# Attention scores of two heads in the two row halves of TensorE, the gate copied out of PSUM, and operand stacks written through DRAM

## What is computed

```python
q, k, v = proj(Wq, bq, layernorm(x)), proj(Wk, bk, ctx), proj(Wv, bv, ctx)
q, k = rope(q, d_rope), rope(k, d_rope)          # the first 8 of each head's 16 channels are rotated
scores = jnp.einsum('bhqd,bhkd->bhqk', q, k) / jnp.sqrt(jnp.float32(kc))
p_attn = jax.nn.softmax(scores, axis=-1)
out = jnp.einsum('bhqk,bhkd->bhqd', p_attn, v)
x = x + proj(Wo, bo, out)
# feed-forward on layernorm(x)
gate = bitlinear(x, w_gate)                      # 512 -> 2048, act_quant(x) @ ternary weights
up = bitlinear(x, w_up)
intermediate = jax.nn.silu(gate) * up
return h_bitlinear(intermediate, w_down)         # Walsh-Hadamard over 2048, act_quant, 2048 -> 512
```

## Time and profile before

| | |
|---|---|
| time, median of 3 runs | 1619.53 us (1617.6 to 1630.68) |
| profiled execution, its own time | 1624.36 us |
| its span, first to last instruction | 1622.6 us |
| busy over the span | TensorE 91%, VectorE 81%, ScalarE 69%, GpSimd 52% |
| mean granted TensorE clock | 0.971 of full speed; full from about 180 us on |
| share of the DMA engines | about 0.3 |

### The profile page before, as it was taken

The page is one execution under the profiler, slowest core; times in us unless marked ns, Lnnn a source line. Parts: engine busy times, 40 slices in busy tenths (PEclk is TensorE's granted clock), DMA queues, the critical chain, the costliest instruction groups (busy, mean ns, idle before and its releaser), DMA issues.

```text
span 1622.6 us, 26340 instructions
## 1 busy us (share of the span) xinstructions
PE 1481.5 (91%) x8579; PEld 666.8 (41%) x8674; DVE 1318.3 (81%) x2317; ACT 1125.9 (69%) x1841; POOL 848.4 (52%) x648
## 2 busy tenths in 40 slices
PE   1378999999999999999999999999999999999984
PEld 0112344444444444444444434444444444444433
DVE  4477988888888888888888888888888888888741
ACT  4436677777777777777777777777777777777662
POOL 0111665555556655555556655555566555555464
PEclk9568999999999999999999999999999999999997
DMA  5633312233333233223332322323332322333000
GB/s 195 167 111 59 56 44 56 54 57 57 66 66 64 42 59 59 55 56 62 66 66 46 60 56 55 58 56 66 66 64 42 63 53 56 57 50 53 14 7 14
DMA packets 79750, 99.50 MB, mean 61 GB/s; under 512 B 9472, under 2 KB 59904, under 8 KB 78592
## 3 DMA queue, kind: packets, MB, share of 16 engines
q1 hardware_dynamic: 79056, 93.62, 30.1%
q10 hardware_dynamic: 560, 4.19, 0.7%
HBM read 38.80 MB, written 8.39 MB: 29 GB/s over the span
## 4 chain that ended last, share of the span: by engine, by line
PE 75%; DVE 12%; issue 3%; POOL 3%; ACT 2%; DMA 2%; SPq 1%; POOLq 0%; DVEq 0%; ACTq 0%
PE pv L468 15%; PE s L453 14%; PE ring L498 13%; PE s L425 12%; PE ring L543 6%; PE ring L397 6%; PE ring L519 4%; DVE maxima L989 3%; PE ring L477 2%; PE ring L530 2%; DVE h_res L1020 1%; DVE st L1022 1%; DVE attn L1009 1%; DVE turned_pv L999 1%; POOL region L1222 1%
## 5 line engine op out<-in xcount | busy, mean ns | idle before, releaser
L989 DVE TENSOR_REDUCE maxima<-s 128x1 bf16<-128x512 f32 x1024 | 667.0, 683 | 119.9 <-PE s L425 117.8
L688 ACT ACTIVATE region<-s 128x512 f32<-128x512 f32 x1024 | 575.2, 597 | 208.1 <-PE s L453 167.4
L1221 POOL TENSOR_TENSOR region<-region 128x512 f32<-128x512 f32 x192 | 253.3, 1319 | 391.3 <-DVE region L1069 363.8
L425 PE MATMUL s<-region 96*128 96x512 bf16 x1024 | 374.0, 390 | 26.0 <-DMA region<-parts 15.8
L453 PE MATMUL s<-region 97*128 97x512 bf16 x1024 | 352.8, 384 | 5.5 <-ACT region L688 3.0
L468 PE MATMUL pv<-region,v_ext 128*32 128x512 f32 x2048 | 267.2, 605 | 0.5 <-DVE turned_pv L999 0.4
L1222 POOL TENSOR_TENSOR region<-region 128x512 f32<-128x512 f32 x192 | 245.4, 1278 | 0.0
L453 PEld LDWEIGHTS s<-region 97*128 97x128 bf16 x1024 | 95.9, 98 | 240.0 <-ACT region L688 121.2
L425 PEld LDWEIGHTS s<-region 96*128 96x128 bf16 x1024 | 97.6, 97 | 205.8 <-DVE maxima L989 74.7
L1256 POOL TENSOR_TENSOR region<-region,parts 128x1024 f32<-128x1024 f32 x32 | 68.1, 2129 | 175.1 <-ACT parts L755 175.1
L704 ACT ACTIVATE region<-ring 128x512 f32<-128x512 f32 x128 | 76.2, 596 | 116.1 <-PE ring L509 116.1
(11 more groups left out here) (113 smaller groups left out, 1858.1 us busy)
## 6 DMA issues: line engine op xcount, KB each, us to landing
region<-parts SPq DMA_DIRECT2D x768, 64.0 KB
x_in<-in_x SPq DMA_DIRECT2D x32, 256.0 KB, 2.6
c_in<-in_ctx SPq DMA_DIRECT2D x32, 256.0 KB, 2.9
x_res<-in_x SPq DMA_DIRECT2D x32, 256.0 KB, 4.0
out<-o_sb SPq DMA_DIRECT2D x32, 256.0 KB, 4.1
region<-in_wg_t ACTq DMA_DIRECT2D x1, 2048.0 KB, 10.6
region<-in_wu_t SPq DMA_DIRECT2D x1, 2048.0 KB, 7.4
region<-in_wd_t SPq DMA_DIRECT2D x1, 2048.0 KB, 14.8
```

Of the source, the lines that this page charges most:

```text
L425: pe.matmul(s1[p][:, :], q_stack[k][0:STACK, h, 128 * c:128 * (c + 1)], k_stack[k][0:STACK, h, :], start=True, stop=True).then_inc(s1_full ...
L688: act.activation(probs[:, n % 8, :], s2[n % 2][:, :], ACT.Exp, scale=SCALE).then_inc(exp_done, 1)
L989: dve.reduce_max(maxima[:, c, h:h + 1], s1[p][:, :], AXX).then_inc(s1_max[p], 1)
L1221: pool.tensor_tensor(o[:, :, 0, :], a[:, :, 0, :], a[:, :, 1, :], ALU.add)
```

## The change

**Row halves.** The heads are paired, an even one (p = 0) and an odd one (p = 1). Its operands lie in rows 0 to 63 for the even and in rows 64 to 127 for the odd head. 64 rows hold four of the six terms (main); the other two terms and the maximum lie in 33 rows of a second column block (rest). `score_max(b, i)` is now a pair of matmuls with 64 rows each, one for each head, into both banks `s1`; it uses the four main terms. `scores(b, m)` is a pair over the main rows and a pair over the rest rows that accumulates onto it, into both banks `s2`. A pair waits until both banks have been read. There are 16 of each a unit.

**Gate.** ScalarE copies a quarter of the gate out of PSUM (`gate_out`), VectorE's `glu` multiplies only up with 1 + tanh, and GpSimd multiplies the two (`gate_product`).

**Stacks.** SP writes each part to a DRAM tensor `scratch` (6 DMAs a unit) and reads from there (12 DMAs a unit, 6 main and 6 rest) into the stacks.

**Weights and order.** up is loaded beside gate, into other buffers. Rounding is on VectorE (one instruction a piece) and the ternary step is ScalarE's Sign; the two steps of clipping are gone. All lists `step(t)` are new, and so is the ring's order.

```diff
-            def score_max(b, n):
-                if not live(b):
-                    return
-                k, p, i = slot(b), n % 2, n // 2
-                h, c = 2 * (i // KC) + p, i % KC
-                if n == 0:
-                    pe.wait_ge(stacked, 16 * STACK_DMAS * (b + 1))
-                wait(pe, s1_max[p], 16 * b + i)
-                pe.matmul(s1[p][:, :], q_stack[k][0:STACK, h, 128 * c:128 * (c + 1)],
-                          k_stack[k][0:STACK, h, :], start=True, stop=True).then_inc(s1_full[p], 1)
+            def score_max(b, i):
+
+                if not live(b):
+                    return
+                k, c = slot(b), i % KC
+                if i == 0:
+                    pe.wait_ge(main_stacked, 16 * READS_MAIN * (b + 1))
+                for p in range(2):
+                    wait(pe, s1_max[p], 16 * b + i)
+                j = i // KC
+                for p in range(2):
+                    pe.matmul(s1[p][:, :], q_stack[k][main_rows(p), j, 128 * c:128 * (c + 1)],
+                              k_stack[k][main_rows(p), j, :], start=True, stop=True).then_inc(s1_full[p], 1)
...
-            def scores(b, n):
+            def scores(b, m):
...
+                k, u = slot(b), m // 2
+                j, c = 2 * (u // KC) + m % 2, u % KC
...
-                wait(pe, exp_done, 32 * b + n - 1)
-                pe.matmul(s2[n % 2][:, :], k_stack[k][0:STACK + 1, h, 128 * c:128 * (c + 1)],
-                          q_stack[k][0:STACK + 1, h, :], start=True, stop=True).then_inc(s2_full, 1)
+                wait(pe, exp_done, 32 * b + 2 * m)
+                for p in range(2):
+                    pe.matmul(s2[p][:, :], k_stack[k][main_rows(p), j, 128 * c:128 * (c + 1)],
+                              q_stack[k][main_rows(p), j, :], start=True, stop=False)
+                j += PAIRS
+                for p in range(2):
+                    pe.matmul(s2[p][:, :], k_stack[k][rest_rows(p, 1), j, 128 * c:128 * (c + 1)],
+                              q_stack[k][rest_rows(p, 1), j, :], start=False, stop=True).then_inc(s2_full, 1)
...
-                free(f"gate{j}", dve.scalar_tensor_tensor(th[:, j % 2, :], th[:, j % 2, :], 1.0,
-                                                          bank(f"gate{j}")[:, :], ALU.add, ALU.mult))
-                full(dve, f"up{j}", b)
-                moved(dve, f"gate{j}", b)
-                free(f"up{j}", dve.tensor_tensor(z[:, 512 * j:512 * (j + 1)], th[:, j % 2, :],
-                                                 bank(f"up{j}")[:, :], ALU.mult))
+                t = th[:, j % 2, :]
+                free(f"up{j}", dve.scalar_tensor_tensor(t, t, 1.0, bank(f"up{j}")[:, :], ALU.add, ALU.mult))
...
+            def gate_out(b, j):
+                if not live(b):
+                    return
...
+                act.wait_ge(tanh_done, 4 * b + j + 1)
+                free(f"gate{j}", act.activation(z[:, 512 * j:512 * (j + 1)], bank(f"gate{j}")[:, :], ACT.Copy))
...
+            def gate_product(b, j):
+                if not live(b):
+                    return
+                moved(pool, f"gate{j}", b)
+                moved(pool, f"up{j}", b)
+                zj = z[:, 512 * j:512 * (j + 1)]
+                pool.tensor_tensor(zj, zj, th[:, j % 2, :], ALU.mult).then_inc(glu_done, 1)
...
-                for w, (terms, dst) in enumerate(((Q_TERMS, q_stack[k]), (K_TERMS, k_stack[k]))):
-                    for r in range(len(terms)):
-                        if terms[r] == part:
-                            for half in range(2):
-                                row = DH * r + ROPE * half
-                                sp.dma_start(dst[row:row + ROPE, :, :], parts[64 * w:64 * (w + 1), part, half, :]) \
-                                  .then_inc(stacked, 16)
...
+                for half in range(2):
+                    sp.dma_start(scratch[b % 2, :, :, part, half].rearrange("w p d h n -> (w p) (d h) n"),
+                                 parts[:, part, half, :]).then_inc(written[part], 16)
...
+            def read_main(b, p):
...
+                q, key = (scratch[b % 2, w, p].rearrange("t a d h n -> t (a d) (h n)") for w in range(2))
+                lo = main_rows(p).start
+                both = key[0:2].rearrange("t r n -> (t r) n").unsqueeze(0).to_broadcast([2, 2 * DH, PAIRS * T])
+                for part in range(2):
+                    sp.dma_start(q_stack[k][lo + 32 * part:lo + 32 * (part + 1), 0:PAIRS, :],
+                                 q[part:part + 1].to_broadcast([2, DH, PAIRS * T])).then_inc(main_stacked, 16)
+                sp.dma_start(k_stack[k][main_rows(p), 0:PAIRS, :], both).then_inc(main_stacked, 16)
...
-                mix(t - 2, 0)
-                third_part(t)
-                mix(t - 2, 1)
-                hadamard_last(t - 3, 1)
-                rstd1(t + 1)
                 rstd2(t - 2)
+                gate_product(t - 2, 0)
+                gate_product(t - 2, 1)
                 hadamard_half(t - 2, 0)
+                gate_product(t - 2, 2)
                 rest(t + 1)
+                gate_product(t - 2, 3)
                 hadamard_half(t - 2, 1)
+                mix(t - 1, 0)
                 hadamard_last(t - 2, 0)
+                hadamard_last(t - 2, 1)
+                mix(t - 1, 1)
+                rstd1(t + 2)
+                third_part(t + 1)
...
-                stack_part(t + 1, 1)
-                stack_part(t + 1, 2)
-                stack_max(t)
-                load_consts(t + 2)
-                load_weights(t + 2, 1, 0)
-                load_weights(t + 2, 1, 1)
-                load_weights(t, 2, 1)
-                load(t + 3)
-                load_residual(t)
-                load_late_consts(t + 2)
-                store(t - 3)
-                load_weights(t + 1, 2, 0)
-                stack_part(t + 2, 0)
+                load_consts(t + 1)
+                load_late_consts(t + 1)
+                stack_max(t - 2)
+                write_part(t, 0)
+                read_rest(t - 1, 0)
+                read_rest(t - 1, 1)
+                write_part(t, 1)
+                read_main(t, 0)
+                read_main(t, 1)
+                store(t - 4)
+                load(t + 2)
+                load_residual(t - 1)
+                write_part(t, 2)
```

More of the change, by code:

```diff
@@ L48, in slot, with place, main_rows, rest_rows @@
     return b % 3
+def place(h):
+    return NH // 2 * (h % 2) + h // 2
+def main_rows(p):
+    return slice(64 * p, 64 * p + MAIN)
+def rest_rows(p, maxima=0):
+    return slice(64 * p, 64 * p + REST + maxima)
+def max_row(p):
+    return slice(64 * p + REST, 64 * p + REST + 1)
+PAIRS = NH // 2
 def uses(name, b):
@@ new lines, in read_main, with read_rest @@
+                sp.dma_start(k_stack[k][main_rows(p), 0:PAIRS, :], both).then_inc(main_stacked, 16)
+            def read_rest(b, p):
+                if not live(b):
+                    return
+                k = slot(b)
+                for i in (0, 2):
+                    sp.wait_ge(written[i], 32 * (b + 1))
+                    sp.nop(nofuse=True)
+                if p == 0:
+                    wait(sp, rest_stacked, 16 * READS_REST * b)
+                    sp.nop(nofuse=True)
+                    wait(sp, s2_full, 32 * (b - 2))
+                    sp.nop(nofuse=True)
+                    unstaged(sp, b)
+                    sp.nop(nofuse=True)
+                q, key = (scratch[b % 2, w, p].rearrange("t a d h n -> t (a d) (h n)") for w in range(2))
+                lo = rest_rows(p).start
+                sp.dma_start(q_stack[k][lo:lo + DH, PAIRS:NH, :], q[2]).then_inc(rest_stacked, 16)
+                sp.dma_start(q_stack[k][lo + DH:lo + REST, PAIRS:NH, :], q[0]).then_inc(rest_stacked, 16)
+                sp.dma_start(k_stack[k][rest_rows(p), PAIRS:NH, :], key[0:3:2]).then_inc(rest_stacked, 16)
@@ new lines, in step @@
+                up_sum(t - 1)
+                down(t - 4, 8, 12)
+                score_max(t - 1, 10)
+                scores(t - 2, 13)
+                weigh(t - 2, 5)
+                score_max(t - 1, 11)
+                scores(t - 2, 14)
+                down(t - 4, 12, 16)
+                score_max(t - 1, 12)
+                scores(t - 2, 15)
+                weigh(t - 2, 6)
+                score_max(t - 1, 13)
+                weigh(t - 2, 7)
+                z_transpose(t - 3, 0)
+                project_v(t)
@@ new lines, in step @@
+                xq_transpose(t - 2)
+                score_max(t, 1)
+                scores(t - 1, 0)
+                gate_up(t - 2, "gate", 0)
+                gate_up(t - 2, "up", 0)
+                scores(t - 1, 1)
+                gate_up(t - 2, "gate", 1)
+                gate_up(t - 2, "up", 1)
+                scores(t - 1, 2)
+                gate_up(t - 2, "gate", 2)
+                score_max(t, 2)
+                scores(t - 1, 3)
+                gate_up(t - 2, "up", 2)
+                weigh(t - 1, 0)
@@ new lines, in step @@
+                scores(t - 1, 4)
```

(18 more changed lines are left out.)

533 lines of the change are left out of this document (246 added, 287 removed).

## The result

The kernel after the change takes 2304.2 us (median of 4 runs, 2303.7 to 2320.5), the kernel before 1621.1 (1617.6 to 1630.7): ratio 1.4225, 95% interval 1.414 to 1.431. The forecast was 1632 us, at most 1690.

A forecast was written before the change was run, and what follows sets the result against it. TensorE's own sequence was taken to set the period of 45.96 us. 31 periods x 0.64 = +20, start -12, end +5 gave +13 against the median of 1619.5: 1632 us, range 1562 to 1690.

The forecast's parts named there:

- Stacks by way of DRAM: SP's writes and reads through scratch: 8 issues with two hops about 10.5 us, needed 14 later, 3 us of cover.
- cover under 1 us: Maxima's two DMAs: land some 3 us after the maxima's transposition, score step 0 comes 4 us after it.
- TensorE's terms: TensorE's sequence: halves of a pair run at once, each change of shape costs 0.10, bare work falls 0.7 us a unit.
- rivals 1 and 2: 1: shape changes into row halves free, 1568 us, 0.20; 2: halves overlap partly, 1690, 0.07, or not, 1900 to 1950, 0.04.
- rival 4: TensorE's savings and shape changes cancel, waits hidden: period stays 45.96, 1612 us, at the forecast's lower edge; no separate chance.
- The period of 46.6: One steady-state unit after the change, summed over three stretches: 46.6 us against 45.96, +0.64 a unit.
- a: Unit from pair 1 to pair 8: TensorE is the bound, 25.2 us including 26 changes of shape.
- b: Unit from pair 8 to pair 13: seams of the reductions bare, five pair loops of 1.80, 9.0 us.
- (c): Pair 13 to pair 1 of the next unit: a chain through VectorE, 12.4 to 13 us, taken as 12.4.
- bare pair loop: Maxima's score pair, its two reductions on VectorE and their hand-overs in a row: 1.80 us.
- Rival 3: GpSimd's in-order queue becomes the bound, free only 0.1 before: period about 48.1, 1678 us; 0.25 together with missed waits.
- Start and end: Start -12 us (0 to -25), first score pair near 43; end +5 (3 to 8) from GpSimd's products.

The follow-up runs named there:

- e1: Kernel after the change, its main stack reads reordered so that the long dimension (16 rows) comes first, eight reads instead of six: 1796.1 us, ratio 1.107.
- e5: e1 with the maxima's DMAs and the third part's write issued right behind the main reads, ahead of the four 256 KB transfers: 1667.5 us, ratio 1.029.
- e7: e5 with xn's normalisation on VectorE moved behind the reduction that it had stood ahead of: 1656.1 us, ratio 1.021.

## Why the prediction was wrong

**The step that failed** is in "Stacks by way of DRAM": "8 issues with two hops take about 10.5", with the hop at the 2.6 us of an input DMA. That input has 128 rows on its first dimension; these reads have 2, and the last of them took 22.24 where the sum has 2.6. With the long dimension first they took 2.8 (e1). From the end of the second part to the matmul that waited for it were 30.8 us (1046.57 to 1077.39), less 16.3 of wait: the cover was 14.5, as forecast (14), and as the same paragraph says, each us too late costs one. The text named a cover, "3 us", and gave the reads no upper end, so neither range nor rivals held a transfer of 22 us. In the accounts of one unit, 67.7 against e5's 47.1: 16.3 at pair 0, 2.0 at score step 0, and 2.3 by difference. The timelines show where these 2.3 lie: from score pair 0 to the same quarter of up are 11.00 us in the kernel after (1077.39 to 1088.39) and 6.72 in e5 (721.42 to 728.14), 4.28 more, of which 2.04 are the second wait. The other 2.24 are matmuls at the lower clock: it was granted at 0.50 from 1077.4 to 1080 and at 0.55 from 1085 to 1088.

**The maxima's "cover under 1 us"** was right as a warning and wrong as a cost of nothing. What used it up was not the second DMA but the queue: with narrow reads, and still with wide reads, they follow four 256 KB transfers. e1 to e5: 128 us, of which the waits for `region<-neg_max` in e1 are 73. The lower clock behind them can account for most of the rest: it was granted at 0.64 for 4.4 us in the unit shown (1036.6 to 1041.0), which over 30 such waits makes 48 us by estimate.

**TensorE's terms held.** In the kernel after, the two matmuls of a pair start together (one row, x2, 0.39 for both, as long as one alone) and the next pair follows in 0.21 to 0.23: the exponentials' main pair behind the maxima's (1045.46, 1045.67), the rest pair behind that (1045.90). From the rest pair to the next full-width matmul it is 0.31 instead of 0.22 (1044.06 to 1044.37): 0.09 a change, forecast 0.10. So rivals 1 and 2 are both out, and rival 4 with them, since the period of e5 isn't 45.96. Rows of the kernel after:

```profile
1044.06 0.38 PE L538 MATMUL s<-region 33*128 33x512 bf16 x2
1044.37 1.04 PE L628 MATMUL ring<-wd,y_last 128*128 128x512 bf16 x4
1045.46 0.39 PE L503 MATMUL s<-region 64*128 64x512 bf16 x2
1045.67 0.39 PE L534 MATMUL s<-region 64*128 64x512 bf16 x2
1045.90 0.38 PE L538 MATMUL s<-region 33*128 33x512 bf16 x2
```

The period of 46.6 was forecast; with the DMAs mended it is 47.11. The three stretches of the forecast are in e5 25.1 us (a: 724.14 to 749.22), 9.3 (b: to 758.48) and 12.8 (c: to 771.26), forecast 25.2, 9.0 and 12.4: a bare pair loop takes 1.85 and not 1.80, and (c) comes at the upper part of its "12.4 to 13". Once xn no longer stands in front of a reduction (e7) the period is 46.66. That this is the forecast's 46.6 is chance: the forecast had xn in its place. **Rival 3** (GpSimd's order) didn't come about: in e5 the mix of (c) waits for VectorE's reciprocal, not in GpSimd's queue, as the prediction's list of signs had it. GpSimd was free 0.24 before, forecast 0.1:

```profile
761.02 0.62 POOL L1331 TENSOR_TENSOR mixed<-turned_pv,inv_sum 128x256 f32<-128x256 f32 x1 [0.24 <-DVE inv_sum L1085]
```

**Start and end.** -12 was forecast for the start; e5's first output projection is at 143.6, before's at 144.7, -1. Its first score pair runs at 58.38 instead of 43, after 12.70 us of waiting for the unit's stacks from DRAM, which nothing covers at the start: while the weights load, the write's landing takes 6.98 us and the last read's 7.10. In the kernel after that wait is 31.84. From the last output projection to the end it is 59.5 in e5 and 57.1 before: +2.4 (forecast +5). But the second period (53.5 for 48.9) and the last two (89.4 for 83.0) grew by 11 together, which the forecast hadn't. With 28 periods of 1.1 these make e5's +43.

So the mechanism on TensorE was read rightly from the trace, and the sum failed on a transfer that was priced by another transfer's landing without asking how many DMA engines its shape would use. Even with the DMAs mended the change stays some 2% slower than before, and slower in each period, as the forecast of +0.64 us a unit had it in direction.

## What to carry to other kernels

Before a DMA is priced by a row of another, compare the first dimension of both: a zero-stride copy or an index of 2 in front left 14 of 16 engines idle here, and moving it behind the rows cost two more issues a unit and gave back 508 us. In a profile the sign is a low DMA share together with long landings. And small DMAs on which an engine waits belong in front of the large ones in their queue; a wait with "cover under 1 us" is a term of the range, not a zero.

## What the runs showed of the hardware

- Narrow DMAs slow others that are issued behind them on the same queue and don't touch their data: landings of `c_in` went from 15.5 us after the change to 4.6 with wide reads (e1), those of `out` from 21.3 to 2.7. The issuing queue itself stalls: one issue of `out` took 5.26 us in the kernel after and 0.71 in e1.
- Behind a wait of 2.4 us TensorE's clock went to the lower level in e1 (1.89 us for four matmuls that otherwise take 1.04; granted 0.64 over the 4.4 us behind the wait, 1.00 again from 1041 us); in a unit of e5, whose longest wait was 0.67, it stayed at 1.00.
- A pair of matmuls in the two row halves takes the time of one, and a change between row halves and full width costs 0.09 us.
- Four engines' worth of 1 KB packets (the writes) moved 81 GB/s, two engines' worth of 4 KB packets 51.
